# Indirect writes of slot rows: one series at the end of a slot, or one at a time over the next slot

## Time and profile before

| | us |
|---|---|
| median of 3 runs (lowest, highest) | 1904.03 (1899.94, 1919.91) |
| the profiled execution's own time | 1913.67 |
| its span in the trace | 1911.9 |
| PE busy in the span | 1504.1 (79%) |
| DVE busy | 947.1 (50%) |
| ACT busy | 684.9 (36%) |
| POOL busy | 497.4 (26%) |
| POOL, indirect writes of `a` (64) and `c` (64) | 63.4 and 63.7 |
| mean granted PE clock over the span | 0.875 |

### The profile page before, as it was taken

One profiled execution on the slowest core, in us unless ns is written; L12 is line 12 of the kernel. 1 busy time (PEld: TensorE's weight loads), 2 busy tenths in 40 slices (PEclk: granted clock), 3 DMA queues, 4 the chain that ended last, 5 costly groups with the idle time before them and its releaser, 6 DMA issues. The chain is left out here.

```text
span 1911.9 us, 31286 instructions
## 1 busy us (share of the span) xinstructions
PE 1504.1 (79%) x10329; PEld 967.5 (51%) x10330; DVE 947.1 (50%) x3644; ACT 684.9 (36%) x953; POOL 497.4 (26%) x418
## 2 busy tenths in 40 slices
PE   3688888797888649999379999999996288888870
PEld 1245444354444426666135555555554277777760
DVE  3657776656666511111457686767433433233325
ACT  1143443343434511110145676666753122221212
POOL 4022323313233411122110213221212333333330
PEclk8698878787788869999689999999987599999995
DMA  6744444335232123441154553355253233333324
GB/s 158 184 97 83 101 99 103 75 84 118 63 75 71 54 62 85 114 118 28 39 110 100 116 124 97 73 121 122 65 164 125 70 54 55 55 55 55 55 42 182
DMA packets 117551, 174.49 MB, mean 91 GB/s; under 512 B 17031, under 2 KB 100385, under 8 KB 110256
## 3 DMA queue, kind: packets, MB, share of 16 engines
q1 hardware_dynamic: 94224, 147.65, 31.6%
q0 software_dynamic: 20928, 23.56, 7.5%
q10 hardware_dynamic: 2272, 1.66, 0.3%
HBM read 107.27 MB, written 72.82 MB: 94 GB/s over the span
## 5 line engine op out<-in xcount | busy, mean ns | idle before, releaser
L834 ACT ACTIVATE arena<-ST 128x1024 f32<-128x1024 f32 x416 | 414.9, 1024 | 338.7 <-PE ST L701 322.3
L1093 DVE CUSTOM_DVE_ANT_0 scratch<-shared,mask 128x512 bf16<-128x512 f32 (+3 forms) x512 | 229.0, 487 | 125.5 <-PE shared L810 98.9
L701 PE MATMUL ST<-arena 96*128 96x256 bf16 (+2 forms) x1792 | 260.6, 283 | 16.0 <-DMA arena<-qk_parts 13.6
L719 PE MATMUL OT<-arena,v_aug 128*32 128x256 f32 (+1 forms) x3584 | 263.0, 396 | 3.9 <-POOL arena L1161 2.7
L701 PEld LDWEIGHTS ST<-arena 96*128 96x128 bf16 (+1 forms) x1792 | 162.9, 104 | 121.0 <-issue 50.3
L810 PE MATMUL shared<-arena 96*128 96x512 bf16 (+3 forms) x512 | 133.1, 340 | 57.0 <-DVE mx L1093 28.7
L1892 POOL DMA_INDIRECT sum<-arena,block_token x72 | 113.9, 1582 | 245.5 <-ACT arena L1848 175.1
L1161 POOL TENSOR_SCALAR_AFFINE_SELECT arena<-arena 128x512 f32<-128x512 f32 (+1 forms) x96 | 78.6, 818 | 316.7 <-ACT arena L834 316.7
L719 PEld LDWEIGHTS OT<-arena,v_aug 128*32 128x32 f32 x3584 | 87.1, 113 | 122.2 <-issue 71.5
L1798 PE MATMUL shared<-arena 128*128 x576 | 136.3, 380 | 0.0
L1848 ACT ACTIVATE arena<-shared,block_gain 128x256 f32<-128x256 f32 x72 | 34.1, 473 | 264.6 <-DMA sum<-arena,block_token 259.2
(11 more groups left out here) (205 smaller groups left out, 2292.2 us busy)
## 6 DMA issues: line engine op xcount, KB each, us to landing
arena<-qk_parts SPq DMA_DIRECT2D x224, 128.0 KB, 7.1
qk_parts<-qk_src SPq DMA_DIRECT2D x64, 384.0 KB, 2.6
arena<-qk_parts SPq DMA_DIRECT2D x32, 384.0 KB, 4.6
block_rows<-slot_x SPq DMA_DIRECT2D x72, 130.0 KB, 2.1
arena<-qk_parts SPq DMA_DIRECT2D x32, 256.0 KB, 5.4
sum<-x_out SPq DMA_DIRECT2D x16, 512.0 KB, 2.9
arena<-in_experts_inter SPq DMA_DIRECT2D x7, 1024.0 KB, 6.9
arena<-in_experts_out SPq DMA_DIRECT2D x7, 1024.0 KB, 9.9
```

The source lines that it names most:

```text
L701: mm = pe.matmul(ST[n % 2][:, i * 256 + at:i * 256 + at + nq], K[par][0:rows, h, kb * P:(kb + 1) * P], Q[par][0:rows, h, q0:q0 + nq], star ...
L719: mm = pe.matmul(OT[32 * i:32 * i + 32, q0:q0 + nq], v_aug[par][:, kb, g * GH + i, :], PT[n % RING][:, i, at:at + nq], start=(u == 0), sto ...
L834: act.activation(PT[n % RING][:, :, :], ST[n % 2][:, :].rearrange("p (h n) -> p h n", h=GH), func, scale=ATT_SCALE).then_inc(L["exp"], 1)
L1093: taken = dve.tensor_tensor_reduce(out=junk[n % 2][:, at:at + m], in0=bank[:, at:at + m], in1=mask[:, 0:m], scale=1.0, scalar=LOW, op0=ALU ...
```

## The change

The writes of batch s-2 are no longer issued in slot s. They are issued in slot s+1 as steps `s3` 0 to 7 (batch s-3, none while that is below 0). `among` lays the eight steps between the `others` of `y`, `ln`, `xp`, `rT`, `lg` and `l1` (in a body or seventh slot of `c`: `y`, `ln`, `xp` and the whole projection), by weight, at ninths of the total. The save, `xs` 3 and `sv` 3, is moved behind all of them: in a body slot of `a` from behind `ln` to behind `qk` and `qs` of the first half, in a body slot of `c` from behind `ln` (ahead of `xl`, the load of the next batch) to the end of the projection; between `s3` 7 and `xs` 3 stand there only `av`, `v` and `st_q` steps, none of which is ACT's. The residual step `xp` stays where it was. The ninth slot has the writes of both of the last batches: `s3` between its steps and `s2` in one series at its end.

```diff
+def among(steps, few, weight):
+    whole = sum(weight.get(step, 0) for step, _ in steps)
+    out, at, done = [], 0, 0
+    for step in steps:
+        out.append(step)
+        at += weight.get(step[0], 0)
+        while done < len(few) and at * (len(few) + 1) >= whole * (done + 1):
+            out.append(few[done])
+            done += 1
+    return out + few[done:]
...
-    save = ([("xs", 3), ("sv", 3)] if route else []) + ([("xp", 0)] if attn else [])
+    save = [("xs", 3), ("sv", 3)] if route else []
+    residual = [("xp", 0)] if attn else []
...
-    scatter = [("sc", i) for i in range(2 * TB)] if route else []
+    scatter = [("s3", i) for i in range(2 * TB)] if route else []
+    last_scatter = [("s2", i) for i in range(2 * TB)] if kind == "ninth" else []
...
     if not prep:
-        others = y + norm + save + rows + route_1 + route_2 + route_3 + scatter + last_save
+        others = (among(y + norm + residual + rows + route_1, scatter, cost) + save + route_2 + route_3
+                  + last_scatter + last_save)
...
-        rest = ([("v", 0), ("v", 1)] + start + y + norm[0:NORM_FIRST] + load[1:] + norm[NORM_FIRST:] + save + load[0:1]
-                + rows + route_1 + halves[0] + route_2 + route_3 + scatter + halves[1])
+        rest = (among([("v", 0), ("v", 1)] + start + y + norm[0:NORM_FIRST] + load[1:] + norm[NORM_FIRST:] + residual
+                      + load[0:1] + rows + route_1, scatter, WEIGHT)
+                + halves[0] + save + route_2 + route_3 + halves[1])
...
-            others = (y + project[0:1] + norm[0:6] + project[1:3] + norm[6:12] + project[3:4] + norm[12:18] + project[4:6] + norm[18:] + save + load
-                      + project[6:] + mixed(combine, rows + route_1 + route_2 + route_3) + scatter)
+            others = (among(y + project[0:1] + norm[0:6] + project[1:3] + norm[6:12] + project[3:4] + norm[12:18]
+                            + project[4:6] + norm[18:] + residual + load + project[6:], scatter, cost)
+                      + save + mixed(combine, rows + route_1 + route_2 + route_3))
...
-                    elif step == "sc":
-                        k, par, half = turn.batch(2)
+                    elif step in ("s2", "s3"):
+                        k, par, half = turn.batch(int(step[1]))
+                        if k < 0:
+                            continue
```

More of the change, by code:

```diff
@@ L209, in spread_out @@
     route_3 = (before_sums + [("ps", 0)] + pieces("l3", n3)) if route else []
-    scatter = [("sc", i) for i in range(2 * TB)] if route else []
+    scatter = [("s3", i) for i in range(2 * TB)] if route else []
+    last_scatter = [("s2", i) for i in range(2 * TB)] if kind == "ninth" else []
+    cost = COST[causal]
     combine = pieces("cb", N_COMBINE)
@@ L246, in spread_out @@
         if not route:
-            start = save
+            start = residual
             n = PROJECT_FIRST[kind]
@@ L262, in spread_out @@
     n_units = NG * per_group
-    cost = COST[causal]
     total, at = sum(cost.get(step, 0) for step, _ in others), 0
```

## The result

The changed kernel takes **1950.32 us** (median of 4 runs, 1940.69 to 1955.68), the kernel before, run beside it, 1905.88 (1899.94 to 1919.91). The ratio is **1.0221**, 95% interval 1.0175 to 1.0268: slower by 33 to 51 us. The forecast was 1907, no change, with a range that ended at 1936. The profiled execution took 1948.58 us with a span of 1946.8, against 1913.67 and 1911.9: 34.9 us longer in the trace. The mean granted clock is the same, 0.874 against 0.875. Ratios and their intervals are taken from fast runs alone; beside the experiments of group 2, 21 of the 31 runs of the kernel before counted as slow, so there a ratio is not the quotient of the medians.

What follows compares the result with a forecast made beforehand. PE was taken to set the pace in `c`, and holes in PE's row to be the question in `a`. Terms -22 - 9 + 23 + 8 + 3.4 = +3, carried to the median 1904.03, gave 1907 us, range 1877 to 1936.

Steps and rivals of the forecast that it cites:

- The series is broken up in `a`: Ends of body slots of `a`: each of PE's five holes falls to about 0.81 us, 22 us gained.
- rival 1: Holes of `a` stay, being caused by something else at the slot's end, such as stack DMAs: 1938 us, chance 0.22.
- The clock in `a`: Body slots of `a`: the low clock behind PE's longer holes goes with them, 9 us gained, bounds 0 and 18.
- POOL's work in `a`: Stage `a`: eight write issues now between masks make a mask at most 1.3 us later, taken as 0.
- The save in `c`, a new wait: Slots 3 to 6 of `c`: ACT's save waits for the last write, PE stops 5.7 us each, 23 us lost.
- The clock in `c`: Slots 3 to 6 of `c`: half clock behind each new PE hole, 8 us lost, bounds 0 and 16.
- The seventh slot of `c`: The save now stands ahead of the `rT` copies that PE's router matmuls wait for: 2.4 us lost.
- the eighth: Eighth slot of `c`: 1.7 us of ACT ahead of a sigmoid near the end, 1 us lost.
- Rival 2: The save in `c` finds its writes landed, so no new wait there: 1876 us, chance 0.18.
- Rival 3: POOL issues in groups of two to four, bringing some 10 us of holes back in `a`: 1917 us, chance 0.08.
- the upper bound of 8.2 us a slot: Body slots of `c`: PE's stop at the new wait if issuing amid DVE's work takes longer, against 5.7 taken.

Runs made afterwards that it cites:

- group 2: The second group of follow-up experiments, on series or place and wait or spreading; the kernel before, run beside it, had a median of 1919.09 us.
- the late save: The changed kernel with the save in `c` (ACT's scaling, SP's store) put behind the combining and routing: 1887.66 us, ratio 0.9803; again 1892.24 us, 0.9937.

## Why the prediction was wrong

The forecast put both effects in the right place and with the right sign; their sum came out at +3 where the traces show +35 and the runs +44. Three terms failed, each by 6 to 10 us in the same direction: the gain of the body slots of `a`, its eighth slot, and the new wait in `c`.

1. **"The series is broken up in `a`", -22: a failed step, too large by 10 us.** The mechanism was right: the hole follows the series (it stays at the slot's end with the old series, goes to the start when the series goes there, is gone when the writes come apart), so rival 1 falls. But the step took each hole to shrink to the 0.81 of `c`, with nothing in its place. Over the body slots PE's idle time fell by 12.0 us, from 69.5 to 57.5; in the ten other traces of kernels with the same body slots of `a` it is 55 to 63. Holes of 2.0 us for `o_nat` came in slots 3 to 6, which stand in every trace without the hole at the slot's end and in neither the kernel before nor the one with the save moved and the writes not. Behind the groups of three came 1.0 to 1.7 us a slot more.
2. **"The clock in `a`", -9: right in this trace.** PE's busy time for the same matmuls fell by 8.5 us. In the ten other traces it fell by 10 to 22, so this term moves from execution to execution; with the first step the body slots gained 20.5 us here and 17.4 to 30.9 there, where -31 was forecast.
3. **"POOL's work in `a`", 0: a failed step.** In the body slots nothing speaks against 0. In the eighth slot there are no projections to keep PE going while a mask waits behind a write, and that slot grew by 6.0 us, 2.6 of it PE's idle time and the rest PE's busy time at a lower clock (0.80 in place of 0.85). I had looked at the eighth slot's ACT in `c` and at the ninth slots, and not at the eighth of `a`. Putting its writes ahead of the attention takes 5.8 us back. The seventh slot grew by 3.1 to 64.1; the kernel with the old series and the save moved has 64.1 too, so that isn't the writes. Nor is the 4.3 us between the stages shown to be: the kernel with the save moved and the writes not has 378.6 too.
4. **"The save in `c`, a new wait", 4 x 5.7 = 23: the mechanism was right and the term too small, a failed step too.** The queue behind ACT's wait, the slots that pay and the engine that stops are those foretold. The holes are 8.1 us, 32.6 in all. The step priced the landing at 2.1 us by the earlier trace rows and misread that row: the trace of the kernel before records no landing of the 128 writes to the slots. The row's median is that of reads of the slot rows in stage `d` (54 of 72 are recorded), its 18.9 the first fill of `slot_x`. The same trace has the landing at the four places where ACT waited for a last write: 2.2 us twice in `a`, and 4.9 and 2.8 at the end of `c` (below). At the new place it is 4.7, 2.6 more than priced, and the holes are 2.4 longer, 9.6 us in the four. POOL's way to the last write was foretold to the tenth, 5.0 us.
5. **"The clock in `c`", 8: right.** For the same 2016 matmuls of the four slots PE is busy 244.7 us, against 237.9 in the kernel before and 235.8 with the late save: 7 to 9 us more, at a clock of 0.93 in place of 0.97 and 0.98.
6. **"The seventh slot of `c`", 2.4, and the eighth, 1.** 3.2 and -1.7 by the slot lengths.

The price that the step could have taken from the kernel before: timelines of POOL and ACT at the end of `c`, and a window from the issue to ACT's start, with a DMA share of 0.86:

```profile
1467.91 0.97 POOL L1630 DMA_INDIRECT slot_x<-x_out,row_to  x1 [0.30 <-issue]
...
1472.77 1.70 ACT L596 ACTIVATE x_out<-x_out,keep 128x256 f32<-128x256 f32 x4 [10.97 <-DMA slot_x<-x_out,row_to]
...
1467.91:1472.77 4.86, 0.00 (x0) 0.00 (x0) 4.08 (x22) 0.00 (x0) 0.97 (x1) 0.98 0.86 318
```

So `c` was forecast at 34 us in all and cost 40 in this trace (49 in the four slots of the changed kernel's second trace against those with the late save). In `a` and up to `c` the forecast had 31 us gained and the trace has 9. Of the 22 that are missing some 10 are the body slots, 6 the eighth slot, and 6 are stretches where no edit was shown to be the cause, nor was it for the 3.5 us behind `c`. The two stages measured apart don't settle these last: 0.9855 times 1.0174 is 1.003, where the whole change is 1.020 to 1.022. The kernel before moved by 0.8% from group to group; against 1905 us the same two medians would give 1.027.

**Rivals.** Rival 2 (writes landed in time) didn't occur, but it is what the late save makes of the kernel: 1887 to 1892 us in the runs, where the rival said 1876. Rival 3 has the right size for `a`, some 10 us of idle time come back, and only part of the reason: a group of three goes with PE's semaphores up to 2.9 us late, and the holes behind it were 1.0 to 1.7 us a slot; the rest is the holes for `o_nat`. Rival 1's time, 1938, is the nearest to the measured one by luck, since its mechanism, that the holes of `a` stay, did not occur.

**Pages.** By the Trainium skill, page "SBUF — State Buffer", section "SBUF: two separate sides", an indirect write issued amid certain VectorE instructions could have waited 2.5 us longer, an estimate from its 620 and 3100 ns. The changed kernel's trace shows no such wait, and nothing in it tells whether the instructions that the page means ran beside the issues: its issues in `c` took 0.99 us in the median and 1.26 at most (tile `slot_x`, ns, minimum, median, maximum):

```profile
L1653 POOL DMA_INDIRECT slot_x<-x_out,row_to x48: 969/987/1261, 1081.5 to 1470.4; - x48
```

So the page pointed at the term that failed, and the reason was another; the upper bound of 8.2 us a slot, worked out with it, is near the measured 8.1 by luck. The same section's rule that PE is never held up is one the runs here don't bear out in effect: three kernels whose stage `a` differs only in where and how closely POOL issues its writes have PE's hole in three places. What carries the effect, whether PE's own work or only the news of it, the traces don't tell.

**What stays open.** Where the rest of the 8.5 us of landing comes from when the last write stands ahead of the last rotation: a third of the store gives 7.3, the load moved behind it 6.8, and both together weren't tried. How much of the 0.3 to 2.4% of the late save is the chip's. And why the `o_nat` holes come when the hole at the slot's end goes.

## What to carry to other kernels

When work is moved later, list what waits for it and where its new wait falls: here the same delay of the writes paid in one stage and cost PE 8 us a slot in the other, because ACT's save hadn't moved far enough. Where a hole is to go, ask which wait ends next: of 22 us of holes 12 were gained. Put the waiting step behind the longest stretch of other work in the slot, not right behind the last thing that it waits for. Price a DMA's landing by a wait for the same kind of DMA, under the traffic of the place where it will be issued, which a window's DMA share shows; a tile's row of landings mixes all the DMAs that touch the tile. And look at a first and a last slot by themselves: what covers a delay in the body slots isn't there.

## What the runs showed of the hardware

- Indirect writes that POOL issues back to back, 0.97 us each with 0.30 between, go with PE's semaphores moving late (in the trace's semaphore events, against the end of the matmul): up to 6.2 us beside eight (kernel before, slot 5 of `a`), 2.9 beside three (late save, slot 3), under 0.5 beside writes that stand apart (one behind each mask, slot 3).
- How long a write of the same size takes from issue to the start of the ACT step that waits for it goes with the other traffic. In the kernel before it was 4.9 us at a DMA share of 0.86 and 2.8 at 0.18, both at the end of `c`. At the last write's new place in `c` it was 4.7, and 2.6 with a third of the store beside it; in the changed kernel's seventh slot, which has no load of x, 3.1. Right behind the load and a store it took 8.5; a third of the store gave 7.3 there and the load moved away 6.8. Issued 5 us earlier against ACT, it landed 1.3 us earlier.
- Behind each of the four holes of 8 us PE was granted 0.50, that is 1.2 GHz, for its first 3.4 to 4.0 us of work; in slot 4, until 1204.7 us.
